# A recommendation tower on one core: gathers tied to TensorE's steps, ids in padded lines, a second-layer tile moved in memory, and another order behind the last gather

## The reference

```python
e = jnp.stack([tbl_0[ids[:, 0]], ..., tbl_25[ids[:, 25]]], axis=1)
all_emb = jnp.concatenate([bottom_output[:, None, :], embeddings], axis=1)
gram = jnp.einsum('bfd,bgd->bfg', all_emb, all_emb)
z = gram[:, _TRIU_I, _TRIU_J]
h = jnp.concatenate([z, r_bottom_output], axis=1)          # 479 wide
h = jnp.maximum(h @ W_top1 + b_top1, 0.0)                   # 512
h = jnp.maximum(h @ W_top2 + b_top2, 0.0)                   # 256
y = h @ W_top3                                              # 1
```

## Time and profile before

| what | value |
|---|---|
| median of 3 runs | 498.77 us (496.91 to 505.03) |
| profiled execution, first to last instruction | 370.7 us |
| the profiled execution's own time | not listed; the median lies 128.1 us above its span |
| PE busy | 343.2 us (93%) |
| POOL busy | 257.2 us (69%) |
| DVE, ACT busy | 236.3 us, 230.8 us |
| DMA | 66.86 MB, 180 GB/s |

### The profile page before, as it was taken

One profiled execution on the slowest core, in us unless ns is written; L12 is line 12 of the kernel. 1 busy time (PEld: TensorE's weight loads), 2 busy tenths in 40 slices (PEclk: granted clock), 3 DMA queues, 4 the chain that ended last, 5 costly groups with the idle time before them and its releaser, 6 DMA issues.

```text
span 370.7 us, 8525 instructions
## 1 busy us (share of the span) xinstructions
PE 343.2 (93%) x3422; PEld 282.3 (76%) x3422; DVE 236.3 (64%) x312; ACT 230.8 (62%) x298; POOL 257.2 (69%) x261
## 2 busy tenths in 40 slices
PE   6899999999699999999999999997977996899996
PEld 5688888887587778788788877776866785677886
DVE  2999999999497769798789945313340332522452
ACT  2699989888497896499997833447321473223222
POOL 5777878777777777777877877777777777770010
PEclk9699999999699999999999999999896999899999
DMA  6977687665957789988767629534593425323200
GB/s 174 249 217 211 194 248 222 190 198 163 319 112 251 205 242 341 287 235 252 230 156 245 191 77 347 176 96 114 152 366 99 115 74 146 97 52 85 66 20 2
DMA packets 48391, 66.86 MB, mean 180 GB/s; under 512 B 15861, under 2 KB 34847, under 8 KB 47840
## 3 DMA queue, kind: packets, MB, share of 16 engines
q1 hardware_dynamic: 40024, 49.32, 43.9%
q0 software_dynamic: 8064, 16.31, 16.7%
q10 hardware_dynamic: 264, 0.69, 0.6%
HBM read 52.36 MB, written 13.93 MB: 179 GB/s over the span
## 4 chain that ended last, share of the span: by engine, by line
PE 69%; POOL 10%; DMA 6%; ACT 5%; issue 5%; DVE 3%; SPq 1%; ACTq 0%; DVEq 0%
PE acc L624 21%; PE acc L625 21%; POOL rows L591 10%; PE gram L655 9%; PE turned L637 6%; PE acc L660 4%; PE acc L661 4%; PE acc L662 4%; DMA rows<-in_tbl,index 2%; DMA wanted<-in_onehot_ids 2%; DVE onehot L899 2%; ACT features L741 1%; ACT staged L823 1%; ACT h L769 1%; DMA square<-products 1%
## 5 line engine op out<-in xcount | busy, mean ns | idle before, releaser
L591 POOL DMA_INDIRECT rows<-in_tbl,index x248 | 253.9, 1024 | 77.7 <-issue 74.4
L899 DVE TENSOR_SCALAR onehot<-wanted,row_number 125x1029 fp32r<-125x1029 int32 (+3 forms) x137 | 151.0, 1150 | 19.6 <-PE acc L625 13.3
L624 PE MATMUL acc<-onehot,table_hi 125*128 125x512 f32 x336 | 136.6, 407 | 3.1 <-DVE table_lo L893 3.1
L625 PE MATMUL acc<-onehot,table_lo 125*128 125x512 f32 x288 | 115.7, 402 | 0.0
L624 PEld LDWEIGHTS acc<-onehot,table_hi 125*128 125x128 f32 x336 | 64.7, 193 | 17.8 <-DVE table_lo L893 3.3
L655 PEld LDWEIGHTS gram<-features 128*54 128x54 f32 x2048 | 60.6, 136 | 17.6 <-issue 14.6
L655 PE MATMUL gram<-features 128*54 128x52 f32 x2048 | 67.5, 222 | 6.0 <-DVE features L925 3.0
L625 PEld LDWEIGHTS acc<-onehot,table_lo 125*128 125x128 f32 x288 | 55.7, 194 | 12.4
L769 ACT ACTIVATE h<-wanted,row_number 125x1029 f32<-125x1029 int32 x42 | 48.8, 1163 | 23.4 <-PE acc L625 20.3
L637 PE MATMUL turned<-identity,rows 128*128 128x128 f32 x248 | 41.8, 294 | 9.9 <-DMA rows<-in_tbl,index 8.1
L772 ACT ACTIVATE onehot<-h,row_number 125x1029 fp32r<-125x1029 f32 x42 | 48.6, 1157 | 1.4
(11 more groups left out here) (49 smaller groups left out, 285.4 us busy)
## 6 DMA issues: line engine op xcount, KB each, us to landing
wanted<-in_onehot_ids SPq DMA_DIRECT2D x20, 514.5 KB, 6.0
parked<-staged SPq DMA_DIRECT2D x32, 256.0 KB, 4.3
table_raw<-in_tbl SPq DMA_DIRECT2D x17, 448.0 KB
looked<-parked SPq DMA_DIRECT2D x2, 2816.0 KB, 12.4
square<-products SPq DMA_DIRECT2D x62, 84.5 KB
rows<-in_tbl,index POOLq DMA_INDIRECT x248
looked<-parked SPq DMA_DIRECT2D x1, 2560.0 KB, 11.0
pairs<-in_tbl SPq DMA_DIRECT2D x3, 448.0 KB
```

What stands on the lines that cost most here:

```text
L591: pool.indirect_dma_start(out=rows[:, n % ROWS_RING, i, :], out_offset=None, in_=gathered[f], in_offset=bass.IndirectOffsetOnAxis(ap=index ...
L624: pe.matmul(to, table_hi[0:ROW_PARTS, v % HIGH_RING, c, :], of, start=(c == 0), stop=False)
L625: last = pe.matmul(to, raw_table(v, low=True)[0:ROW_PARTS, c, :], of, start=False, stop=(c == CHUNKS - 1))
L899: return dve.tensor_scalar(column[:, rows], ids_of(v, slice(0, ROW_PARTS))[:, rows], row_number[0:ROW_PARTS, c:c + 1], None, ALU.is_equal)
```

## The change

Four edits. **(1)** Before each group of gathers, GpSimd waits until TensorE has ended a certain step: the last lookup or Gram chunk that, by the planner's clock, ends 10 us or more before the group's gathers begin. The first five groups have none. From group 1.1 on all 59 have one: 1.1 and 1.2 wait for lookup 0, 15.0 for gram 13.1, 15.1 and 15.2 for gram 13.3, 15.3 for gram 14.0. **(2)** The ids lie in HBM with the pitch of SBUF, so a load writes one run of 4144 bytes to a partition (for the first visit 2368 and 1776). **(3)** `h2` lies in the memory of `table_hi`. VectorE no longer waits in its layer2 step; it waits before it first overwrites `h1_hi` of the next part, and the split of pairs waits for the first layer, not for the output. **(4)** The tail of ORDER is rearranged, layer2 of part 2 is cut in two halves, and part 4 loads its pairs of tile 14 apart from those of tile 15.

```diff
+GATHER_LANDS = 38
+PACE_LEAD = 100
+APART = BLOCKS - 2
+def outputs_of(part, i):
+    return (i,) if part == APART else tuple(range(M2))
...
+    def begun(part):
+        return [("layer1", part, 0)]
+    def rest(part):
+        return [("layer1", part, m) for m in range(1, M1)] + [("layer2", part, 0)]
...
-            before += [[] for _ in range(LAYERS_AT[b] - LOOKUPS_AMONG[b])] + layers(b - 1) + [[("output", b - 1, 0)]]
+            before += [[] for _ in range(LAYERS_AT[b] - LOOKUPS_AMONG[b])] + layers(b - 1)
+            before += [[("output", b - 1, 0)]] if b - 1 != APART else []
...
+    steps += [("layer2", APART, 1)]
     for part in range(BLOCKS - 1, len(PARTS)):
-        steps += [step for place in layers(part) for step in place] + [("output", part, 0)]
-    return steps
+        steps += begun(part) + [("output", part - 1, 0)] + rest(part)
+    return steps + [("output", len(PARTS) - 1, 0)]
...
+        begins.append(gathered - GATHER_LANDS)
...
+        while step == ("layer2", APART, 0) and turns:
+            turn()
...
+        if step[0] in ("lookup", "gram"):
+            ended.append((now, step))
+    for begin in begins:
+        paces.append(max(((end, step) for end, step in ended if end <= begin - PACE_LEAD), default=(0, None))[1])
...
-PAIRS_AFTER["gram", TILES - 2, TILE_CHUNKS - 1] = (len(PARTS) - 2, 0, BLOCK_TILES - 1)
+PAIRS_AFTER["layer1", APART, M1 - 1] = (len(PARTS) - 2, 0, EARLY_TILES)
+PAIRS_AFTER["gram", TILES - 2, TILE_CHUNKS - 1] = (len(PARTS) - 1, EARLY_TILES, BLOCK_TILES - 1)
...
-        table_hi = sb("table_hi", [P, HIGH_RING, CHUNKS, D], F32R)
+        h2_and, table_hi = sb_as("h2", "table_hi", [P, HIGH_RING, CHUNKS, D])
-        h2 = [staged_and[:, :, :, 1 + m, :] for m in range(M2)]
+        h2 = [h2_and[:, m, 0:BLOCK_TILES].rearrange("p q (s t) -> p q s t", s=PACK) for m in range(M2)]
...
-                    sp.dma_start(ids_of(v, slice(0, P)), onehot_ids[i:i + 1, first:first + WIDTH].to_broadcast([P, WIDTH])
-                                 ).then_inc(wanted_landed[v % WANTED_RING], 16)
+                    sp.dma_start(to, of.to_broadcast([P, ID_LINE])).then_inc(wanted_landed[v % WANTED_RING], 16)
...
+            def keep_pace(n):
+                if PACES[n] is None:
+                    return
+                kind, x, y = PACES[n]
+                if kind == "lookup":
+                    pool.wait_ge(accumulated, visited(x))
+                else:
+                    pool.wait_ge(grammed, x * TILE_CHUNKS + y + 1)
...
                     at_least(pool, transposed, n - ROWS_RING + 1)
+                    keep_pace(n)
...
-                    dve.wait_ge(accumulated, FILL["output", last_on_tiles_of(part), 0] + 1)
+                    dve.wait_ge(accumulated, FILL["layer1", last_on_tiles_of(part), M1 - 1] + 1)
...
             def split_h1(part, m):
+                if m == 0 and part:
+                    dve.wait_ge(accumulated, FILL["layer2", part - 1, M2 - 1] + 1)
...
-                elif kind == "layer2":
-                    dve.wait_ge(accumulated, FILL["layer2", x, M2 - 1] + 1)
-                    if x < BLOCKS - 1:
-                        split_bottom(x + 1)
+                elif kind == "layer2" and y == 0 and x < BLOCKS - 1:
+                    split_bottom(x + 1)
```

More of the change, by code:

```diff
@@ L49 @@
 WIDE_RING = 6
+ID_LINE = ID_ROWS * ID_PITCH
 FIRST_ROWS = 4
@@ L184, in order @@
     grams = 0
+    begins, ended, paces = [], [], []
     def turn():
@@ L220, in accumulations @@
         if kind == "layer2":
-            for m in range(M2):
+            for m in outputs_of(b, i):
                 number[kind, b, m] = len(number)
@@ L530, in load_pairs @@
                     sp.wait_ge(accumulated, FILL["layer1", last_on_tiles_of(part), M1 - 1] + 1)
-                for i in range(SP_LOADS if part == len(PARTS) - 1 else len(TRIPLES)):
+                for i in range(SP_LOADS if (part, first, end) == LAST_LOT else len(TRIPLES)):
                     load_triple(sp, b, first, end, i, pairs_landed[part % 2])
@@ L817, in relu1, with relu2 @@
                                      bias=b1_sb[:, m:m + 1]).then_inc(acc_out, 1)
-            def relu2(part):
-                for m in range(M2):
+            def relu2(part, ms):
+                for m in ms:
                     fill = FILL["layer2", part, m]
```

40 lines of the change are left out of this document (23 added, 17 removed).

## The result

The changed kernel took **463.98 us** (median of 5, 458.49 to 475.91), the kernel before 498.77 (5 runs beside them, 496.91 to 505.03). The ratio is **0.922, interval 0.912 to 0.932**; by the medians it is 35 us less, where 496 us was forecast, too near to 498.77 to be told from no change. The forecast range, 489 to 502, lies wholly above all five runs. A ratio that has an interval leaves out the slowest executions of each kernel, so it can differ a little from the quotient of the medians.

A forecast was written before the change was run, and what follows sets the result against it. It took GpSimd's gathers to bound the kernel up to 269 us, a late landing to 280.6, then TensorE's program order. Span 370.7 - 0.9 - 0.9 - 0.7 = 368.2 us, plus a constant 128.1, gave 496 us, range 489 to 502.

The forecast's parts named there:

- the sum: Span 370.7 us less 0.9, 0.9 and 0.7 gives 368.2; with a constant 128.1 us outside the span, 496 us.
- the price of the holds: GpSimd's 59 waits on TensorE: each step ends at least 5.3 us before its group begins; cost 0, gain excluded.
- Second wait: Added waits as instructions on GpSimd, 45 ahead of turn 12.1: between 0 and 13.5 us in all, taken as 0.
- the slower rival: GpSimd pays for a second wait before turn 12.1: 501 us at 0.1 us each, 509.8 at 0.30; chance 0.13.
- Ids: Ids in one run land in 4.5 to 5 us, lookups start 2 to 3 us earlier; value 0, covered by gathers.
- Phase of VectorE and GpSimd: Early start shifts VectorE's work against gathers before turn 12.1: entered as 0, spread 2.4 us for eight times in ten.
- a sign of being wrong: Turn 12.1, expected still near 269 us, being off by more than 3 us.
- The tail: TensorE's order from 335.85 us: gains 0.9 us at turns 15.2 and 15.3, 0.9 at part 3's layer1, 0.7 at its output.
- Part 4's pairs: SP issues the last loads near 348 to 350 us, landed by 352, wanted near 355; margin 3 us, cost 0.
- my rivals: GpSimd pays for second waits (chance 0.13); the gathers' chain gets shorter (0.16); the tail does not give its gain (0.11).
- faster: A median below 488.8 us, needing the whole case of a shorter gather chain or a lucky median; chance 0.09.

The follow-up runs named there:

- holds alone: The kernel before with GpSimd's waits on TensorE's steps alone: 478.88 us, against 507.1 for the kernel before, 0.94.
- lines alone: The kernel before with the ids in padded lines alone: 502.89 us, against 507.1 for the kernel before, 0.99.
- fixed pauses: Clearings after each gather in the changed kernel: two without GpSimd's waits, 449.3 us; one with a wait for each gather, 400.52; kernel before 374.32.
- two pauses: Changed kernel without GpSimd's waits, two short clearings of an unused tile after each gather: 449.3 us, 1.206 of the kernel before.
- three: Changed kernel without GpSimd's waits, three short clearings of an unused tile after each gather: 492.01 us, 0.97 of the kernel before.
- plain rows: Changed kernel without waits, GpSimd issuing plain transfers of each table's first 128 rows in place of gathers: 354.71 us, 0.70 of the kernel before.

## Why the prediction was wrong, and where it was right

**The step that failed** is in the sum: "With the 128.1 us by which the median exceeds the span (498.77 - 370.7) taken as constant". In every run since, time exceeds span by about 1.8 us (470.83 and 469.0 late, 372.63 and 370.8 on time). The 128 us were not around the span; they were inside the spans of executions that the trace does not resemble. The late span of before is 506.0 - 370.7 = 135.3 us longer: TensorE is idle for 112.7 us instead of 27.5 (85.2) and busy for 393.3 instead of 343.2 (50.1), at a clock of 0.865 instead of 0.963. I had the sign of it in my own table, a quarter of the median outside the trace, and treated it as a constant instead of as a sign that the trace is not one of the timed executions.

**What hung on it** is the price of the holds: "in this execution no gather is held", "Cost of holding: 0", "a gain is excluded, since nothing is taken away from POOL". A gain was put at nothing because POOL gets no faster; that it can come from TensorE, which others then answer sooner, was not considered. The first of the three is true of that execution: in the changed kernel's on-time trace the least slack is 5.2 us, at group 15.0, where I had 5.3. The line that answers to the earlier trace rows there:

```profile
L628 POOL DMA_INDIRECT rows<-in_tbl,index x248 | 256.6, 1035 | 77.6 <-issue 72.5 <-DMA index<-in_ids 2.3 <-PE gram L692 1.8
```

In the late ones GpSimd's gathers end 38 to 78 us ahead of their turn in the kernel before, from the third group on. In the changed one it is up to 70 us early on and 6 to 28 us for the last 16 groups; where a hold binds, it is about 0.8 us from TensorE's end to the gather (longer where late). Their value is some 28 us (holds alone). The gain is not the saved idleness only: against the late trace of before, the span of the changed kernel's late trace is 37.0 us shorter, of which TensorE's idle time is 112.7 - 90.5 = 22.2 and its busy time 393.3 - 378.5 = 14.8, at a clock of 0.898 for 0.865.

**The other terms**, held against the changed kernel's on-time trace (span 370.8), where they can be read:
- *Second wait.* Gaps ahead of groups with both waits are 0.30 or 0.31 us; the 1.8 us above are six such gaps. Price 0, as entered; the slower rival did not occur.
- *Ids.* 518 KB land in 3.9 us where the earlier trace rows has 6.0; I expected 4.5 to 5. The first lookup starts at 9.64, not 10.57: 0.9 us, not 2 to 3 (and not before 9 us, as I had said), since `table_lo` is the later of its two conditions. Value 0 stands (and 0.99 of before with lines alone, late, within its scatter).
- *Phase of VectorE and GpSimd.* The mean gather took 1035 ns for 1024: 248 x 11 ns = 2.7 us, just past the 2.4 us entered as spread. Turn 12.1 came at 272.96 instead of 269.49, 3.5 us later, which my own list had as a sign of being wrong (more than 3 us), and the span is 370.8 us, not 368. By the rule of the Trainium skill that I set beside it (SBUF — State Buffer, "Who interferes with whom") the sum would have moved by less than 1 us; one execution cannot decide between them, but 2.7 us is nearer to what the rows gave, and of the 49 gathers here that took more than 1.05 us 30 overlap a `table_lo` operation (26 of 44 in the trace before, by the same count).
- *The tail.* Timeline of PE, the changed kernel on time:

```profile
337.49 1.05 PE L692 MATMUL gram<-features 128*54 128x52 f32 x32
338.47 0.98 PE L674 MATMUL turned<-identity,rows 128*128 128x128 f32 x7
...
342.19 3.56 PE L692 MATMUL gram<-features 128*54 128x52 f32 x128
...
350.10 0.62 PE L738 MATMUL acc<-h,w_sb 128*1 128x128 f32 x16
...
359.43 0.60 PE L738 MATMUL acc<-h,w_sb 128*1 128x128 f32 x8
...
367.96 0.60 PE L738 MATMUL acc<-h,w_sb 128*1 128x128 f32 x8 [0.57 <-ACT h L860]
```

and the last output of the kernel before, from its trace:

```profile
367.80 0.60 PE L701 MATMUL acc<-staged,w_sb 128*1 128x128 f32 x8 [0.57 <-ACT staged L823]
```

Turn 15.2 stands directly behind gram 14.3. The first step of part 3's layer1 takes 350.10 - 348.59 = 1.51 us, for 2.37. Nothing is idle ahead of chunk 15.0 (0.91 in the earlier trace rows) nor ahead of the outputs at 350.10 and 359.43 (0.57 there). From the start of what follows gram 14.3 to the last output's start it is 367.96 - 338.47 = 29.49 us, against 367.80 - 335.85 = 31.95: **-2.46, where I had summed -2.5**. In the late traces it is the same, 466.14 - 436.65 = 29.49 against 503.15 - 471.20 = 31.95. The medians on time agree, -2.5 us; in this one trace turns and gathers had lost 2.6 us before the tail began (338.47 against 335.85).
- *Part 4's pairs.* SP issues the last of them from 350.62 to 352.74, later than the 348 to 350 that I had (350.88 to 352.73 in the earlier trace rows). VectorE splits them from 356.41 on, directly behind its own work for the first layer, and waits for nothing. Cost 0, as entered, with less margin.

So the reading of the trace was right in most of its terms, and the forecast of 496 us wrong, because its difference was worked out for one condition and its level taken from the other. None of my rivals had a case in which TensorE is late; the chance of 0.09 for "faster" came from the gathers' phase, so that the time fell on that side is luck.

## What to carry to other kernels

Before costing an edit, compare the profiled span with the timed runs: they differed by 1.8 to 2.2 us wherever both were of one execution. A surplus of 128 us is no constant, it says that the trace shows another kind of execution, and each "hides it" and "never binds" in it needs a second price for the case that the covered engine is late. Indirect gathers that run far ahead of their use are not always free, even where GpSimd, the bytes and the buffers are (plain transfers that ran ahead were). Tie them to their consumer's progress, evenly, down to the single gather. Such holds cost nothing that could be told with increments on time (ratios of 0.996 to 1.005 for the kernels that have them), while fixed pauses cost 26 to 75 us there.

## What the runs showed of the hardware

- While GpSimd issues indirect gathers at one per 1.25 us, TensorE's increments can reach ScalarE, VectorE, GpSimd and SP late, by 17 us in the late trace of the changed kernel and 25 us in that of the kernel before. They need not: with increments on time the same 248 gathers ran at that spacing in one unbroken row of 332 us (4.01 to 335.90), and nothing was late.
- In late executions, at one gather per 1.35 us, increments still came up to 22 us late; at one per 1.69 us by no more than 1.5 us. With plain transfers of the same size, from GpSimd (at one per 0.53 us) or from ScalarE, none was late while the kernel before, run in turn with them, took 490 to 517 us.
- The rows themselves land on time: the median from the end of a gather's issue to the last of its packets is 1.5 us in the late traces of both kernels, 2.3 in the trace ahead of the prediction. (The Trainium skill, Perfetto Trace Analysis, "DMA Instruction — SWDGE (GPSIMD)", says that the profile's end of such an instruction is the end of descriptor generation, not of the transfer. The traces agree: the first packet follows that end by 0.7 us in the late traces, by 1.0 in the one ahead of the prediction.)
- TensorE also pauses inside its steps, with nothing to wait for: weight loads of Gram chunks wait 64.2 us for "issue" in the late trace of before, 47.7 in that of the changed kernel, 16.1 in its on-time one. That fits a TensorE that is held up in giving its increments off, but no run shows it.
- The granted clock falls with TensorE's idle time, whatever made it: 0.865 with 112.7 us idle and 0.898 with 90.5 (late), but also 0.893 with 91.9 us under two pauses and on time, and 0.865 with 121.6 under three. With 27.5 and 31.4 us it was 0.963 and 0.977, with 18.5 (plain rows) 0.990.
- Open: what puts an execution in one condition or the other (the indirect gathers are needed, since the two kernels without them were never late, but they do not suffice); whether it is their form or their scattered rows; and where between 1.35 and 1.69 us lateness fades.
